# A decoder layer on one core: feed-forward loads begun by GpSimd, bulk loads in parts, projections in halves

## The reference

```python
def bitnet_linear(x, weight, scale_param):
    s = jnp.maximum(jnp.mean(jnp.abs(weight), axis=1), 1e-08)
    y = jnp.einsum('bsi,oi->bso', x, jnp.sign(weight / s[:, None]))
    return jnp.nan_to_num(y * (s * scale_param)[None, None, :], nan=0.0, posinf=1e6, neginf=-1e6)

def _binary_diff_weight(w, base):
    d = w - base
    return base + jnp.mean(jnp.abs(d)) * jnp.sign(d)

# attention: 32 heads of 16 features, 8 key/value heads (each serves 4 query heads), 4 sequences
x = x + attention(layernorm(x))          # q, k, v, o by bitnet_linear, softmax over 512 keys
x = x + down(silu(gate(n)) * up(n))      # n = layernorm(x); W1, W3: 1792 x 512, W2: 512 x 1792
```

## Time and profile before

| | us |
|---|---|
| median of 3 runs | 1049.82 |
| lowest and highest | 1045.49, 1054.92 |
| the profiled execution, whole | 1054.04 |
| its span, first to last instruction | 1052.0 |
| mean granted TensorE clock in it | 0.955 |

### The profile page before, as it was taken

One profiled execution on the slowest core, in us unless ns is written; L12 is line 12 of the kernel. 1 busy time (PEld: TensorE's weight loads), 2 busy tenths in 40 slices (PEclk: granted clock), 3 DMA queues, 4 the chain that ended last, 5 costly groups with the idle time before them and its releaser, 6 DMA issues.

```text
span 1052.0 us, 14162 instructions
## 1 busy us (share of the span) xinstructions
PE 968.0 (92%) x4770; PEld 617.9 (59%) x4770; DVE 736.5 (70%) x978; ACT 538.8 (51%) x999; POOL 293.1 (28%) x247
## 2 busy tenths in 40 slices
PE   3588989999999989898889999999999999999997
PEld 2433433344344433333357888888888888888886
DVE  6585867888888787789695558855687557864443
ACT  3426768877897889574684331332223232232221
POOL 3134767566766642210000110101111110011110
PEclk9858998999999999688999999999999999999999
DMA  4535577455754575511494000240003300130001
GB/s 149 149 127 171 158 150 227 127 146 174 224 153 115 170 224 161 179 45 32 151 303 151 12 1 1 80 148 17 0 0 120 124 0 0 45 116 1 0 0 40
DMA packets 81361, 110.24 MB, mean 105 GB/s; under 512 B 10144, under 2 KB 33696, under 8 KB 81312
## 3 DMA queue, kind: packets, MB, share of 16 engines
q1 hardware_dynamic: 79152, 108.04, 33.8%
q10 hardware_dynamic: 2160, 1.58, 0.5%
HBM read 76.29 MB, written 32.78 MB: 104 GB/s over the span
## 4 chain that ended last, share of the span: by engine, by line
PE 70%; DVE 14%; DMA 5%; issue 3%; ACT 3%; SPq 3%; POOL 2%; DVEq 0%; ACTq 0%; POOLq 0%
PE psum L1389 15%; PE psum L1390 15%; PE psum L1391 14%; DVE nmx L994 8%; PE psum L1308 7%; PE psum L1298 7%; PE psum L1282 3%; DMA q_slot<-shift 3%; DVE g_alt L963 2%; PE psum L1319 2%; PE psum L1320 2%; PE psum L1225 1%; PE psum L1226 1%; ACT probs L832 1%; SPq L454 1%
## 5 line engine op out<-in xcount | busy, mean ns | idle before, releaser
L994 DVE TENSOR_REDUCE nmx<-psum 128x2 f32<-128x1024 f32 x256 | 300.9, 1218 | 74.6 <-PE psum L1282 74.3
L832 ACT ACTIVATE probs<-psum 128x512 f32<-128x512 f32 x512 | 276.1, 604 | 77.1 <-PE psum L1298 74.9
L1298 PE MATMUL psum<-q_slot,k_slot 50*128 50x512 f32 x512 | 172.0, 492 | 16.9 <-DMA q_slot<-shift 13.0
L1389 PE MATMUL psum<-fxh,wh 128*128 128x512 f32 x448 | 175.2, 391 | 2.2 <-DVE wl L1152 2.2
L1390 PE MATMUL psum<-fxl,wh 128*128 128x512 f32 x448 | 174.9, 390 | 0.0
L1391 PE MATMUL psum<-fxh,wl 128*128 128x512 f32 x448 | 174.7, 390 | 0.0
L719 POOL CAST dh<-w2T 128x512 fp32r<-128x512 f32 (+1 forms) x56 | 50.7, 906 | 430.1 <-PE psum L1391 393.5
L1298 PEld LDWEIGHTS psum<-q_slot,k_slot 50*128 50x128 f32 x512 | 77.5, 193 | 132.1 <-ACT probs L832 85.6
L1308 PE MATMUL psum<-probs,v_slot 128*32 128x512 f32 x1024 | 146.4, 646 | 0.7 <-ACT probs L832 0.7
L1282 PE MATMUL psum<-k_slot,q_slot 48*128 48x512 f32 x512 | 115.3, 465 | 26.7 <-DVE nmx L994 24.8
L1159 DVE TENSOR_TENSOR gate<-gate,psum 128x512 f32<-128x512 f32 x56 | 38.4, 686 | 133.6 <-PE psum L1391 131.3
(11 more groups left out here) (109 smaller groups left out, 1272.7 us busy)
## 6 DMA issues: line engine op xcount, KB each, us to landing
stage<-in_L_ffn_mean_w_dram SPq DMA_DIRECT2D x84, 256.0 KB, 4.6
q_slot<-q_stack SPq DMA_DIRECT2D x64, 192.0 KB, 3.5
stage<-in_L_ffn_w_dram SPq DMA_DIRECT2D x42, 256.0 KB, 4.8
q_stack<-q_hi SPq DMA_DIRECT2D x32, 256.0 KB
weighted_values<-u_sb SPq DMA_DIRECT2D x32, 256.0 KB, 3.8
k_slot<-k_stack SPq DMA_DIRECT2D x64, 96.0 KB, 3.6
xn<-_attn_hidden_states_dram SPq DMA_DIRECT2D x4, 1024.0 KB, 6.8
q_stack<-q_lo SPq DMA_DIRECT2D x16, 256.0 KB
```

What stands on the lines that cost most here:

```text
L832: nc.scalar.activation(probs[kt][:, j, :], BANK[ring_bank(("score", g, kt, j))], ACT.Exp, scale=HEAD_DIM ** -0.5).then_inc(exp_ok, 1)
L994: v.tensor_reduce(column, pair, AX.X, ALU.max, negate=True).then_inc(s_max, 1)
L1298: mm(BANK[ring_bank(("score", g, kt, j))], k_slot[s][rows, kt * P:(kt + 1) * P], q_slot[s][rows, jj, :], start=True, stop=True).then_inc(t ...
L1389: mm(o, lhs_hi, rhs_hi, start=first, stop=False)
```

## The change

1. **Loads of differences go to GpSimd's queue**, half a tile a group: the weight half (3 loads) at the first slice of each odd group, the base half at that of each even one; both halves of tile 0 in group 0. The wait for the buffers (magnitudes and signs of tile e - 2) goes with them. `difference` is cut into three operations, at slices 5 + 8e, 6 + 8e, 7 + 8e; each third has its own sign and magnitude.
2. **Magnitudes are summed by ScalarE** (`accum_out` into `dsum`); `add_magnitude`, its 1536-wide accumulator and its initial zeros go.
3. **Items in halves.** In the batches beside attention each item is projected as 256 columns in one slice and 256 in the next, with a scaled copy for each half; guard and selection come one slice later than before, and V is third of six instead of last. TensorE's order in a slice is new: scores 0 and 2, a plain pair, the work beside, a plain pair, scores 1 and 3, then the values; the copy of a group's result (`copy_u`) follows the four exponentials.
4. **Start.** K and V weights come first; only K, one Q tile, V and a second Q tile are projected before the first plain score, the last two Q tiles after plain scores 1 and 3, signs of the o_w weights and the spread of the factors (by transposes of a broadcast column and two copies of ScalarE, `output_signs`) after plain score 6. Group 0's slot is filled from `q_hi` and `q_lo` in SBUF, 12 small loads by SP and 6 by GpSimd. Statistics of batch 1 stand behind maxima 9 to 12, the means behind maximum 13.
5. **Bulk loads in parts** over several groups: tokens in two halves, the residual in two, the weighted values two and two, the reciprocals one and three, base tiles for the feed-forward one in each of the last four groups. The sums of batch 0 are loaded 12 slices before the last batch and inverted 5 before it; attended values at slice 9, output tiles at 15, 19, 23, 27.
6. The factors' store and load through DRAM go.

```diff
-ITEMS = (KTILE, QT, QT + 1, QT + 2, QT + 3, VTILE)
+ITEMS = (KTILE, QT, VTILE, QT + 1, QT + 2, QT + 3)
+VALUES = ITEMS.index(VTILE)
-GUARD_LAG, PRED_LAG = 1, 3
-VT_AT = 24
-INVERT_AT, ATTENDED_AT, PROJECT_AT, PROJECT_EVERY = 4, 10, 16, 4
-DIFF_AT = tuple(range(1, 112, 8))
+GUARD_LAG, PRED_LAG = 2, 4
+VT_AT = 16
+STORE_AT = (8, 12, 16, 20, 24)
+INVERT_AT, ATTENDED_AT = 27, 9
+PROJECT_AT = (15, 19, 23, 27)
+DIFF_AT = tuple(range(5, 112, 8))
...
-        if at in ITEM_AT:
-            return "item", b, ITEM_AT.index(at)
+        for i in range(len(ITEMS)):
+            if 0 <= at - ITEM_AT[i] < 2:
+                return "item", b, i, at - ITEM_AT[i]
...
+    def first_keys(eng, part):
+        src = (q_lo, q_hi, q_hi)[part][0]
+        for h in range(2):
+            r = HALF * h + HEAD_DIM * part
+            eng.dma_start(k_slot[0][r:r + HEAD_DIM, :].bitcast(FP32), src[0:HEAD_DIM].bitcast(FP32)).then_inc(slot_in[0], 16)
...
@@ sp_group @@
-            for e in range(2, IT):
-                if 4 * g - 2 < DIFF_AT[e - 2] + SUM_LAG + 1 <= 4 * g + 2:
-                    load_difference(e)
-            if g == 3:
-                load_factors()
-            if g == 5:
-                spread_factors()
-            if b == BATCH - 1 and at == 0:
+            if b == BATCH - 2 and at == SLICES - 12:
                 for p in range(2):
                     sp.wait_ge(u_out[p], 16 * KV_HEADS // 2)
                 load_sums(0)
@@ gpsimd @@
-        nc.gpsimd.memset(dacc[:], 0.0).then_inc(facc_init, 1)
+        pool.wait_ge(qh_ok, 2)
+        for part in range(2):
+            first_heads(nc.gpsimd, part, 1, first_in)
+        pool.wait_ge(ql_ok, 2)
+        first_heads(nc.gpsimd, 2, 1, first_in)
         pool.wait_ge(v_ok, 1)
         fill_values(0)
...
-        def add_magnitude(e):
-            pool.wait_ge(fabs_ok, 3 * (e + 1))
-            positive(pool, facc_ok, e)
-            nc.gpsimd.tensor_tensor(dacc[:], dacc[:], mn[e % 2][:], ALU.add).then_inc(facc_ok, 1)
+        def load_difference(e, part):
+            if part == 0:
+                if e >= 2:
+                    pool.wait_ge(facc_ok, 3 * (e - 1))
+                    pool.wait_ge(fsgn_ok, 3 * (e - 1))
+                load_tile(nc.gpsimd, e, wn[e % 2], (w1, w3, w2), fw_in[e % 2])
+            else:
+                load_tile(nc.gpsimd, e, mn[e % 2], (m1, m3, m2), fw_in[e % 2])
...
@@ pool_slice, ahead of all else in it @@
+            if kt == 0 and g == 0:
+                load_difference(0, 0)
+                load_difference(0, 1)
+            elif kt == 0 and g % 2 == 1 and g // 2 + 1 < IT:
+                load_difference(g // 2 + 1, 0)
+            elif kt == 0 and g % 2 == 0 and g // 2 < IT:
+                load_difference(g // 2, 1)
@@ act_slice @@
             for j in J_ORDER:
-                if j == J_ORDER[3]:
-                    if kt == 0 and g > 0:
-                        copy_u(g - 1)
-                    if beside(g, kt):
-                        beside_out(beside(g, kt))
+                if j == J_ORDER[2] and beside(g, kt):
+                    beside_out(beside(g, kt))
...
-                    nc.scalar.activation(mn[e % 2][:, k - 3, :], wn[e % 2][:, k - 3, :], ACT.Abs).then_inc(fabs_ok, 1)
+                    nc.scalar.activation(mn[e % 2][:, k - 3, :], wn[e % 2][:, k - 3, :], ACT.Abs,
+                                         accum_out=dsum[:, k - 3, e:e + 1]).then_inc(facc_ok, 1)
@@ vector, ahead of the groups @@
-        for i in range(TT):
-            token_stats(1, i)
-        token_means(1)
         for nn in range(S_AHEAD):
             maxima(nn)
+            if nn in (1, 3):
+                guard(4 + nn // 2)
+                lo_item(4 + nn // 2)
+            if nn == 4:
+                weight_scales(2)
+                output_scales(slice(OT, WTILES))
             if nn == 8:
                 split_shift(0)
+            if 9 <= nn < 9 + TT:
+                token_stats(1, nn - 9)
+        token_means(1)
@@ pe_slice @@
             shifted_scores(g, kt, J_ORDER[0])
+            shifted_scores(g, kt, J_ORDER[1])
             if n < S_USES:
                 scores(n)
+            if beside(g, kt):
+                beside_in(beside(g, kt))
+            if n < S_USES:
                 scores(n + 1)
-            shifted_scores(g, kt, J_ORDER[1])
             shifted_scores(g, kt, J_ORDER[2])
+            shifted_scores(g, kt, J_ORDER[3])
             if kt > 0:
                 weigh_values(g, kt - 1)
...
-            if beside(g, kt):
-                beside_in(beside(g, kt))
-            shifted_scores(g, kt, J_ORDER[3])
@@ tensor, ahead of the groups @@
         for nn in range(S_AHEAD):
             scores(nn)
+            if nn in (1, 3):
+                first_item(4 + nn // 2)
+            if nn == 6:
+                output_signs()
```

More of the change, by code:

```diff
@@ L115, in decoder_layer @@
     fac_row = keep("fac_row", [P, 2, KT, P])
+    sums = keep("sums", [P, P])
     dtot = keep("dtot", [P, 3])
@@ L176, in decoder_layer @@
     o_alt = late("o_alt", [P, SEQ])
-    sums = late("sums", [P, P])
     st2 = late("st2", [P, TT, 6])
@@ L368, in ring_free @@
             eng.wait_ge(xe_ok, 4 * (which[0] - 1) + which[1] + 1)
+        elif kind == "item" and which[2] == 0:
+            eng.wait_ge(y0_ok, NI * (which[0] - 1) + which[1] + 1)
         elif kind == "item":
@@ L794, in _ @@
             signs_out(m)
+        for a in range(2):
+            act.wait_ge(fac_mm, a + 1)
+            nc.scalar.activation(fac_row[:, a, :, :].rearrange("p t c -> p (t c)"), BANK[FAC_BANK[a]], ACT.Copy).then_inc(fac_ok, 1)
         def beside_out(user):
@@ L983, in _ @@
             v.tensor_tensor(xl[:, kt, :], BANK[kt], xh[:, kt, :].bitcast(FP32), ALU.subtract).then_inc(xl_ok, 1)
-        for i in range(NI):
-            guard(i)
+        guard(0)
+        lo_item(0)
+        guard(1)
+        lo_item(1)
+        guard(2)
+        guard(3)
+        lo_item(3)
         def maxima(nn):
```

385 lines of the change are left out of this document (230 added, 155 removed).

## The result

The changed kernel takes 1061.66 us (median of 7 runs, 1057.81 to 1066.85) against 1049.82: the ratio of the runs is 1.0126 with a 95% interval of 1.009 to 1.0162 (the two medians alone give 1.0113). It is slower by 1.3%, clear of noise, where the prediction said 1033 us and faster. The profiled execution has a span of 1065.0 us (1052.0 before), 13.0 more. Profiled executions are not medians (1066.85 is the highest of these seven, and the profile of experiment 1 is the lowest of its ten), so two profiles can differ by more than the runs do.

What follows compares the result with a forecast made beforehand. Feed-forward matmuls (43%) untouched; before them VectorE's maxima, attention matmuls, the shift transfer and SP's issuing take turns. Parts A to G, +7 - 7 - 16 - 5 + 11 + 3 - 10 = -17, took 1049.8 to 1033 us; range 1020 to 1043.

Steps and rivals of the forecast that it cites:

- Part A: Start to end of group 1: later batch 1 statistics delay GpSimd's normalisation, less some credits; +7 us (-3 to +15).
- Part B: SP's queue in groups 2 to 7: late shift rows go as difference loads and factors' store leave; -7 us (0 to -9).
- Part C: Half items between scores fill TensorE's bubbles, 0.9 us an item over 18 items; -16 us (-34 to +13).
- Rival 3: Half items: they fill nothing because TensorE has no bubbles, C = 0; 1049 us, chance 0.12.
- Part D: VectorE's masked copies, slow beside GpSimd's L678 and L672, get shorter; -5 us (0 to -8).
- Part E: GpSimd's queue, groups 9 and 17: loads ahead of the token split make TensorE wait; +11 us (6 to 17).
- rival 1: GpSimd becomes the bound at its loads, from 1.7 us a load; 1069 us at 2.0, chance 0.17.
- Part F: ScalarE's accumulator on 42 magnitudes, 0.07 us each, all of it counted; +3 us (0 to +26).
- Part G: Last batch: sums loaded and inverted earlier remove VectorE's wait, low clock and a shift wait; -10 us (-5 to -15).

Runs made afterwards that it cites:

- experiment 1: Changed kernel with GpSimd's difference loads issued after its other work of the slice instead of ahead of it; ratio 1.0026 to the kernel before.
- Experiment 2: Changed kernel with batch 1's token statistics and means behind maximum 6 instead of behind maxima 9 to 13; ratio 1.0033 to the kernel before.
- Experiments 9 and 10: On "halves, old order": 9, difference loads on SP, 0.988; 10, six loads every odd group, on SP 0.9907, on GpSimd 0.9962.
- Experiment 5: Changed kernel with both repairs (experiment 1, Experiment 2): halves/new slice order 0.9883, wholes/new 0.9821, wholes/old 0.9827, halves/old 0.9788.
- experiment 7: "halves, old order" with the accumulator's sum of magnitudes left out; ratio 0.9853 to the kernel before.
- experiment 6: Experiment 5's kernel with halves and new order, but the old order within a slice in groups 24 to 31 alone; ratio 0.9858.
- halves, old order: Changed kernel with both repairs (experiment 1, Experiment 2), half items and the order within a slice of before; 0.9788, median 1028.74 us.

## Why the prediction was wrong, step by step

**Part A, the start: right.** +7 forecast, +7.6 measured, and by its mechanism: first maximum at 42.76 (43 forecast), statistics ended at 75.8 (77), first transpose of batch 1's tokens at 85.61 (87), a wait of 11.00 us for GpSimd's normalisation (8 or more). Experiment 2 confirms it. What I didn't ask is whether the piece could stand elsewhere; three to six maxima earlier group 1 ends 14.6 us sooner.

**Part B, SP's queue: right in its outcome, and by luck.** The waits for the shift are nearly gone. Groups 2 to 7 fell by 7.2, but that holds C, D and F of batch 0's share too, for which I had counted another 4 or 5 (75 was forecast for them, 79.6 came). Experiments 9 and 10 go against the reason given, that the shift rows overtake loads of another queue: with the loads back on SP's queue the shift is no later, and with whole tiles on GpSimd's it is late seven times. What removed the 14.6 us is not isolated: whole tiles on SP's queue, as before the change, leave 3.2 in its one profile, so neither the queue nor the amount seems to account for most of it. The factors' store and the other bulk loads in parts are left, and no run undid these.

**Part C, half items: the first step that failed.** "I take 0.9 us an item, 18 items: -16." The pacing was right: half matmuls stand 0.118 us apart (219.35 to 220.06 for six intervals), and ScalarE's two copies take 0.48 each. What failed is the bubble that the halves were to fill: "quiet slice: 2.75 us, 11.0/4; TensorE's own work in it some 2.1". No row gave the 2.1. The profile of the kernel before has TensorE busy for 10.73 of the 11.0 us of a quiet group, 2.68 a slice, and ScalarE for 9.78 (behind the comma stand PE, PEld, DVE, ACT and POOL):

```profile
402.70:413.70 11.00, 10.73 (x66) 3.97 (x65) 10.04 (x11) 9.78 (x20) 7.08 (x3) 1.00 0.36 94
```

The profile models the ends of matmuls, so the true bubbles can be larger; but 0.07 us a slice was all that it showed, where the forecast counted on 0.65. A half also runs from 219.13 to 220.34, so two take 2.42 where the whole took 2.12, from the first start to the last end. Experiment 5 gives the balance: halves and order together save 1.45 us a batch, 0.24 us an item, then lose 7.7 in the last batch, and side by side the two of them cost 6.6 us in the median where -16 was forecast. Rival 3 (C = 0) named this, and even it was too kind.

**Part D, GpSimd against VectorE: right in kind, too large.** The longest masked copy fell by 1.7 us, as forecast (under 2 us). But six copies are long now where three were. Against 0.75 us each, the three had 8.5 us too much and the six have 6.1, so -5 was not to be had: at most -2.4. No run took it alone.

**Part E, GpSimd's queue: right, and too small.** The wait was forecast at 4.4 us in groups 9 and 17 and is 4.84 in both. The loads cost 0.57 and 0.76 instead of 1.0, but TensorE was there 0.6 us before ScalarE's end and not 0.5 after it. The term that failed is the clock behind it: "1 each" where experiment 1 shows 1.3 and 4.1. So +15.5 for +11. (By the part's own terms its lower bound, with 0.43 a load, is 7.4 and not 6, and rival 1 counts E as +19 where the part has 17.) Rival 1's condition, 1.7 us a load, was never near: a load takes a third to a half of that.

**Part F: too large, inside its range.** +3 forecast, 0.8 shown by experiment 7 in 23 of the 32 groups. The operation costs three times my 0.07 us, but the step "so all of it counts" was wrong: nearly all of it lies beside other work.

**Part G, the last batch: the second step that failed.** "-10" came out as 0. The step's own part held: group 25 fell from 18.6 to 11.4. But "the output tiles keep their VectorE work one slice earlier: nothing" and the want of any next late thing were wrong. Three things came in its place: 3.65 us for the reciprocals, whose remaining three loads SP issues only at 435.35; the granted clock of 0.82 over groups 26 to 31 (0.85 before) behind it; and the new order, 6.0 us in groups 28 to 31 by experiment 5 and 5.5 by experiment 6. I had given the new order no term at all, and it is the term that decides: with the old order and all else of Part G, the late reciprocals included, the last batch takes 107.3, 111.1 and 112.3 us (experiments 5 and 6), 7 to 12 less than the 119.1 before.

**The sum.** By stretches, forecast against shown: start +7 and +7.6; groups 2 to 7 -12 and -7.2; batches 1 and 2 without E's wait -15 and -4 (103.4 and 102.7 in experiment 1 for 105.0 and 105.2); E's wait +11 and +15.5; last batch -10 and 0; feed-forward 0 and +1. The forecasts by stretch add up to -19, two more than the sum of the parts, which I had not noticed; what was shown adds up to +13. Most of the miss is C in three batches: some 12 us by experiment 5, and up to 16 by the stretches, in which B and D lie too. Then come G (10, of which some 6 are the new order that came with C) and E's clock (4.5). None of my rivals was this case: the one on the slow side needed GpSimd to be short of time, while what made the kernel slower was the order in its queue and in VectorE's. The prediction had itself worked these two out at +18, and outweighed them with gains that no row carried.

What stays open: B and D by themselves, and what a stop of TensorE costs behind it. Late keys remain even in the fastest kernel: group 15 of "halves, old order" takes 14.2 us where the kernel with whole tiles on SP takes 11.3, and there a plain score waits 1.41 us for its keys, at a DMA share of 0.90 and a granted clock of 0.76 over the group:

```profile
268.94:283.13 14.19, 10.07 (x23) 0.76 0.90 260
271.97 0.73 PE L1398 MATMUL psum<-k_slot,q_slot 48*128 48x512 f32 x4 [1.41 <-DMA k_slot<-k_stack]
```

## What to carry to other kernels

Costs that a trace gives as a queue's order (what stands behind a waiting instruction, and who waits for that) came out within a microsecond, their clock apart; gains that are "time which now fills bubbles" came out at a quarter where they were meant to fall and as a loss over the whole kernel. Book the first in full and the second near nothing until the length of the bubble itself is a row. A new order of work gets a term of its own, in every stretch in which it runs. And when a wait is removed, look for the next transfer on the same queue: here the sums' wait turned into the reciprocals' wait, and that, moved, into the shift's.

## What the runs showed of the hardware

- A sum by ScalarE's accumulator is not free: an ACTIVATION_READ_ACCUMULATOR of 186 to 243 ns follows each activation.
- A DMA begun by GpSimd occupied it 0.57 us for 256 KB of W1 or W3 and 0.76 us for 256 KB of W2; SP's issues of the base tiles took 0.97 (two in 1.94) and 0.44 in the kernel before.
- Moving bulk loads to another queue did not in itself keep small transfers on time: with 1.5 MB begun at once on GpSimd's queue the shift rows on SP's were late seven times, by up to 2.2 us, and the kernel was slower than with the same loads on SP's own queue (medians of 1046.96 and 1038.77 us); with half of that at once it was 1.7% faster.
- A stop of TensorE of 4.84 us came with the low clock both times, but cost 1.3 us behind it once and 4.1 the other time: the granted clock was 0.82 and 0.76 over the two groups. Two more profiles have 21.6, 19.0, 19.0 and 18.8 us for these groups, which take 12.8 without the stop.
